# The causal mask's product on VectorE, one head later, instead of on GpSimd, in a three-stage vision kernel

## The reference

```python
x = rmsnorm(tokens, norm_w)
q = (x @ Wq)   # 16 query heads of 64
k, v = x @ Wkv # 8 key/value heads of 64: two query heads share one
q, k = l2norm(q) * (q_gamma + 1) * 8, l2norm(k) * (k_gamma + 1) * 8
sim = tanh(q @ k.T / 50) * 50 / 8
sim = where(triu(ones(n, n), 1), -max, sim)      # causal
out = softmax(sim) @ v
x1 = layernorm(tokens + out @ Wout)
```

## Time and profile before

| | us |
|---|---|
| timed runs, median of 3 (lowest, highest) | 2081.14 (2079.12, 2081.46) |
| profiled execution, its own time | 2070.81 |
| span of that execution, first to last instruction | 2069.1 |
| busy: PE, DVE, ACT, POOL | 1838.8, 1195.2, 877.6, 609.9 |

### The profile page before, as it was taken

The page is one execution under the profiler, slowest core; times in us unless marked ns, Lnnn a source line. Parts: engine busy times, 40 slices in busy tenths (PEclk is TensorE's granted clock), DMA queues, the critical chain, the costliest instruction groups (busy, mean ns, idle before and its releaser), DMA issues. The chain is left out here.

```text
span 2069.1 us, 31611 instructions
## 1 busy us (share of the span) xinstructions
PE 1838.8 (89%) x11768; PEld 1586.8 (77%) x11768; DVE 1195.2 (58%) x2023; ACT 877.6 (42%) x1076; POOL 609.9 (29%) x452
## 2 busy tenths in 40 slices
PE   3698898897987998998899899779999999999997
PEld 2598798897976877777787778668787787877876
DVE  6788878888865776777667677421341414314141
ACT  3554554544435664666367366322222222212221
POOL 3212223223150231332122122232433334333332
PEclk9799999998998999999999999889999999999999
DMA  9122311213111000200200020060000000000000
GB/s 120 54 77 97 118 75 53 89 75 145 49 44 50 22 22 9 84 22 15 77 22 15 8 70 22 8 267 1 21 21 0 20 0 20 20 0 21 1 11 11
DMA packets 32213, 95.89 MB, mean 46 GB/s; under 512 B 18630, under 2 KB 18758, under 8 KB 26569
## 3 DMA queue, kind: packets, MB, share of 16 engines
q1 hardware_dynamic: 32076, 94.00, 14.5%
HBM read 81.37 MB, written 24.15 MB: 51 GB/s over the span
## 5 line engine op out<-in xcount | busy, mean ns | idle before, releaser
L573 PE MATMUL conv<-w_hi,x_hi 128*128 128x368 f16 (+5 forms) x1320 | 355.0, 278 | 4.2 <-issue 4.0
L573 PE MATMUL conv<-w_lo,x_hi 128*128 128x368 f16 (+5 forms) x1320 | 355.7, 278 | 0.0
L573 PE MATMUL conv<-w_hi,x_lo 128*128 128x368 f16 (+5 forms) x1320 | 354.4, 278 | 0.0
L835 POOL TENSOR_TENSOR probs<-probs,mask 128x512 f32<-128x512 f32 x128 | 167.3, 1307 | 440.6 <-ACT probs L909 440.6
L1327 ACT ACTIVATE raw_c<-ring,sh 128x512 f32<-128x512 f32 x128 | 88.2, 689 | 371.3 <-PE ring L1424 371.2
L1115 PE MATMUL mixed<-v,probs 128*128 128x65 f32 x1536 | 201.6, 282 | 41.4 <-DVE parts L995 41.2
L1115 PEld LDWEIGHTS mixed<-v,probs 128*128 128x128 f32 x1536 | 185.8, 195 | 56.9 <-issue 40.2
L1289 POOL TENSOR_TENSOR ha_lo<-raw_c,ha_hi 128x512 fp32r<-128x512 f32 x128 | 165.1, 1290 | 210.0 <-DVE ha_hi L1339 210.0
L1424 PE MATMUL ring<-ha_hi,wh 128*128 128x512 f32 x512 | 208.7, 408 | 16.9 <-POOL ha_lo L1289 16.9
L1424 PE MATMUL ring<-ha_lo,wh 128*128 128x512 f32 x512 | 205.2, 401 | 0.0
L1339 DVE CAST ha_hi<-raw_c 128x512 fp32r<-128x512 f32 x128 | 80.7, 631 | 213.2 <-ACT raw_c L1327 211.0
(11 more groups left out here) (153 smaller groups left out, 3757.1 us busy)
## 6 DMA issues: line engine op xcount, KB each, us to landing
xt<-x_columns_in SPq DMA_DIRECT2D x12, 1163.0 KB, 5.2
xp<-x_patches_in SPq DMA_DIRECT2D x12, 1152.0 KB, 8.9
hidden_words<-hidden_weights_in SPq DMA_DIRECT2D x8, 1408.0 KB, 8.7
words<-hidden_words SPq DMA_DIRECT2D x32, 352.0 KB, 3.1
wh<-hidden_words SPq DMA_DIRECT2D x2, 4096.0 KB, 21.2
tokens<-total SPq DMA_DIRECT2D x4, 1024.0 KB, 4.6
lines<-tokens SPq DMA_DIRECT2D x4, 1024.0 KB, 5.5
h<-tokens SPq DMA_DIRECT2D x4, 1024.0 KB, 7.4
```

The source lines that it names most:

```text
L573: ins = pe.matmul(out, xs[:, c, RI - 1 - i:RI - 1 - i + NR, :, x].rearrange("p r g -> p (r g)"), w, start=(t == 0), stop=(t == len(terms) ...
L835: pool.tensor_tensor(diag, diag, both, ALU.mult).then_inc(s_mask, 1)
```

## The change

GpSimd no longer has a part in `score`. VectorE gets a helper `apply_mask(g, n)` with the same product on the same views, in place, and the same increment of `s_mask`. VectorE calls it for head n-1 where its list comes to `score` n (n from 1), so ahead of the normalisation of head n-2 in the same slot (behind it where n is 8, 16 or 24). The mask of the last head is applied ahead of the normalisation of head 30. Before its first step VectorE waits once for the mask tile (`s_const`).

```diff
@@ GpSimd's emit
-                    elif kind == "score":
-                        n = step[1]
-                        pool.wait_ge(s_exp, g * NH + n + 1)
-                        diag = probs[:, n % 4].rearrange("p m (b i) -> p m b i", b=3)[:, :, 0:3:2]
-                        both = mask[:].rearrange("p (m b i) -> p m b i", m=1, b=1).to_broadcast([P, 2, 2, P])
-                        pool.tensor_tensor(diag, diag, both, ALU.mult).then_inc(s_mask, 1)
@@ VectorE
             dve.memset(bits[:], 0).then_inc(s_bits, 1)
+            dve.wait_ge(s_const, 3)
...
+            def apply_mask(g, n):
+                dve.wait_ge(s_exp, g * NH + n + 1)
+                diag = probs[:, n % 4].rearrange("p m (b i) -> p m b i", b=3)[:, :, 0:3:2]
+                both = mask[:].rearrange("p (m b i) -> p m b i", m=1, b=1).to_broadcast([P, 2, 2, P])
+                dve.tensor_tensor(diag, diag, both, ALU.mult).then_inc(s_mask, 1)
+
             def emit(run, g):
                 for step in run.order:
                     kind = step[0]
+                    if kind == "score" and step[1] > 0:
+                        apply_mask(g, step[1] - 1)
+                    elif kind == "mix" and step[1] == NH - 2:
+                        apply_mask(g, NH - 1)
```

## The result

The changed kernel took 2053.89 us in the median of 4 runs (2053.35 to 2060.64), beside 2080.7 for the kernel before (four runs; the prediction had three of them): ratio 0.988, 95% interval 0.9858 to 0.9901; the two medians alone give 0.987. The kernel is faster by 1.2%. The profiled execution took 2053.72 us; the prediction had 2052.6 for it, 2063 for the median, and a range of 2052 to 2078.

The account below looks back on a forecast made before the run. TensorE's order of work plus its waits for VectorE's queue was taken to bound the attention stage. Image terms of -2.7, -5.7, -4.9, -4.9 and nothing gave -18.2 us, so median 2063; range 2052 to 2078.

Parts of the forecast that it names:

- VectorE pays for GpSimd's mask: Attention stage: a VectorE instruction meeting a GpSimd mask stands still until it ends, in the queue TensorE waits for.
- The 58 us of relief: VectorE's standing still that goes with GpSimd's masks: L998 36.5 us, L960 12.5, L954 8.9, together 58 us.
- 0.60 a mask: What each of 128 masks adds to VectorE's queue: 0.60 us, in all 77 us.
- case C: Rival: VectorE's queue gets longer, by masks above 0.60 us or relief under 23 us; 2086 at 1.215 a mask; chance 0.10.
- No new wait through the mask's place: VectorE's mask n-1 in slot n adds no wait: exp is ready, and TensorE already waits for the normalisation behind it.
- The sum: Attention stage's gains added image by image, four groups of up to four images: -18.2 us, profiled execution 2052.6.
- the steady one: Steady image, second of each group and third of the last, 5 in all: about -0.53 us each, -2.7 together.
- I take the same 18 off it: Step from profile to median: the timed median, 2081.14, 10 us above the profiled execution, also falls by 18, to 2063.
- Case A: Rival: denser TensorE work gives back a third of the granted clock's cost, 9 us lower, 2054; chance 0.15.
- Thirty-eight masks on the path: About 38 of 128 masks stand ahead of TensorE's waits, so a microsecond more per mask would cost 38.
- B: Rival: TensorE next waits for ScalarE to empty the banks; only waits at image ends are gained, 2077; chance 0.14.
- D: Rival: VectorE waits for exp at its queue's head, normalisation behind it; 0.15 x 128 = 19 us, 2082; chance 0.06.

Follow-up runs that it names:

- idle product: Changed kernel, with GpSimd also doing a mask-sized product on a spare tile nobody waits for, when exp is done: 2101.6 us, ratio 1.0103 to the kernel before.
- idle memset: Changed kernel, with GpSimd also writing zeros into a spare tile of 1408 columns when exp is done: 2072.4 us, ratio 0.9957 to the kernel before.
- mask twice: Changed kernel, with each mask done twice on VectorE, the second waiting for the first: 2119.5 us, ratio 1.0179 to the kernel before.
- mask behind: Changed kernel, with VectorE's mask behind the normalisation of the same slot instead of in front of it: 2111.8 us, ratio 1.0173 to the kernel before.
- mask at once: Changed kernel, with the mask of head n in slot n itself, one head earlier: 2143.3 us, ratio 1.0317 to the kernel before.
- second root and words: Changed kernel, with only each image's second inverse root on GpSimd and VectorE's or-ing of weight words moved to n = 4, 8, ... 32: 2029.1 us, ratio 0.9771.
- no mask: Kernel before, with the causal mask's product left out on every engine, so attention isn't causal: 2027.1 us, ratio 0.9732 to the kernel before.
- GpSimd later: Kernel before, mask still on GpSimd but started one head later, after the scores of head n+1: 2090.5 us, ratio 1.0049 to the kernel before.
- words moved: Changed kernel, with VectorE's or-ing of the weights' words at n = 4, 8, ... 32 instead of 2, 6, ... 30: 2053.6 us, ratio 0.9865.
- roots on GpSimd: Changed kernel, with both inverse roots of the heads' norms moved from VectorE to GpSimd as maximum and power: 2050.9 us, ratio 0.9863 to the kernel before.

## Why the prediction was right, and where not

**What bounds it:** TensorE's waits for VectorE's queue. Right. Each experiment with longer waits was slower than the changed kernel, and taking them away by other means (the last one) gave the largest gain that keeps the computation whole.

**VectorE pays for GpSimd's mask.** Right, and shown by the idle product, which brings the stops back with nobody waiting for it. But "an instruction of VectorE that meets a mask stands still" was too wide: in the kernel before, `parts`, which reads `mixed` in PSUM, met a mask 59 times and took 424 to 426 ns each time. And L954, which the prediction lists among the instructions with both inputs in SBUF, has one input; "idle memset" shows that it is stopped by GpSimd's writing too. The 58 us of relief came out as (0.575 - 0.292) x 128 = 36, (0.319 - 0.183) x 90 = 12 and (0.477 - 0.178) x 30 = 9.

**0.60 a mask.** Measured 0.61, in place and with a broadcast: case C's first half is out. The start before the end of the instruction ahead is seen at the mask too (0.08 us). It isn't against the Trainium skill: the section that the prediction cites ("VectorE: DVE Perf Modes", "The DRAIN you can't avoid") goes on to say that a next instruction that is not held starts earlier, which the prediction left out.

**No new wait through the mask's place.** Right for the place that was chosen: VectorE waits 12.9 us for exp in 10 places, of which 3.7 is the very first, ahead of which it had nothing to do. The other nine are of 1.0 us, at the first head of an image; only in the last image does a normalisation follow within 3 us. The prediction had found that one place, of 0.15. The two runs with another place, +57 and +88 us, show how narrow that is. The reason I gave, that TensorE's next mixture needs both the mask and the normalisation, would have allowed the place behind as well, for 8 us. What decides is that the mask stands where VectorE would wait for the mixture; the prediction saw this for masks 12 to 14 and did not make it the rule.

**The sum.** From tanh to tanh, the lengths of the four groups were 176.69, 177.49, 177.15 us and 126.8 for the last; they became 170.41, 173.65, 173.63 and 123.8. That is -6.3, -3.8, -3.5 and -3.0, forecast -5.8, -4.7, -5.3 and -2.4: together -16.6 against -18.2. By images of the second group: the first 36.39 to 38.29 (+1.90, forecast -0.92), the steady one 36.11 to 35.16 (-0.95, forecast -0.53), the third 39.97 to 38.15 (-1.82, forecast -1.65), the fourth 65.02 to 62.05 (-2.97, forecast -1.63). The first stood at the lower clock for 6.8 us where it had stood at the higher one throughout, the fourth for 6.8 instead of 10.2; so the sum came out nearer than its terms, which is luck in part. The windows of the first image, before and after:

```profile
829.57:865.96 36.39, 32.42 (x229) 27.14 (x230) 30.50 (x75) 22.80 (x31) 12.25 (x10) 1.00 0.34 118
822.83:861.12 38.29, 35.25 (x229) 29.52 (x230) 30.18 (x82) 22.80 (x30) 1.93 (x2) 0.91 0.32 112
```

The sum was also to come from waits alone. TensorE's waits for the parts were to fall from 41.2 to about 27 us and fell to 33.6; all its waits for VectorE fell by 12.2 in the stretch, its whole idle time by 13.4 (56.6 to 43.2), and the other 3.2 of the 16.6 are busy time (601.5 to 598.3). Ahead of mixture 3 of the second group, 853.30 became 846.21 with the group's start 6.74 earlier: -0.35, forecast -0.42. The profiled execution was to take 2052.6 and took 2053.7. (A slip that changes nothing: the chances of "faster" add up to 0.75 at most, not 0.76.)

**The median.** 2063 was forecast, about 2054 measured: inside the range of 2052 to 2078, but below the 2056 to 2071 that the forecast kept for itself. The step that failed is "I take the same 18 off it". The 10 us between the profiled execution and the median of before were the clock (0.954 against 0.947), and this is not a constant that both kernels carry: the changed kernel ran at 0.952 in the mean, near its profile. Case A had this at 9 us, at a chance of 0.15, with 2054 as its time, and that is what came; it was not a rival to the forecast but rode on it. That shorter waits are what raised the clock is likely by the clocks below, but no run here shows it apart.

**Thirty-eight masks on the path, 38 us for a microsecond.** The count was fair (44 by the waits of "mask twice"), the price was not: a microsecond of TensorE's waiting was followed by about as much in the clock. From the changed kernel, waits and half the low time (an estimate of its cost) against what was added to the profiled execution: idle memset +9 and +11, +17; idle product +24 and +17, +43; mask behind +25 and +24, +54; mask twice +32 and +34, +66; mask at once +48 and +37, +90. Where waits were taken away it doesn't hold: second root and words -22 and -5, -27; no mask -20 and +2, -16. The mean clock over all executions of a kernel says the same: 0.952 for the changed kernel, then with growing waits 0.948 (idle memset), 0.947 (before), 0.944 (GpSimd later), 0.943, 0.939, 0.937 and 0.934 (mask at once); with shorter waits it is 0.951 (words moved), 0.950 (roots on GpSimd), 0.952 (second root) and 0.955 (no mask). Why the clock follows the waits so closely in one direction and less in the other I can't say from these runs. Waits aren't all of it either, as the two profiles of the kernel before show (42.5 and 70.4 us low with waits of 50.3 and 51.4). And the half of the low time counts stretches in which TensorE waited anyway, so the sums are no proof of a mechanism; that more waiting comes with more low clock is what they show.

**B** (the wait moves to ScalarE) and **D** (exp) did not come about in the changed kernel; D's mechanism is real and costs 88 us one head earlier.

## What to carry to other kernels

When an engine with time to spare shares its work with a busy one, look at the busy engine's smallest instructions: a mean well above their shortest record (575 ns against 290) is another engine's work being paid for in the queue that counts, and moving that work onto the busy engine can be cheaper than leaving it. Put added work where the engine would wait for something else, in front of the wait and not behind it; here 57 us lay between the two. And do not build a forecast of a median on a single profile without looking at its granted clock: a wait added to TensorE cost itself and, in these runs, about as much again in the clock; a wait taken away gave back little more than itself.

## What the runs showed of the hardware that I had not expected

GpSimd's writing alone (a memset of 1.27 us) does not touch VectorE's products with two inputs (292 ns) but stops its maximum with one input (500 ns against 178). GpSimd's power with two inputs in SBUF, 4.19 us from 882.67, does not stop VectorE's mask at 883.85, which took its 0.68 us. Nor is it the only one: 15 masks and 45 products `o` lay wholly inside such a power, at 0.68 and 0.29 us. So not every GpSimd instruction that reads SBUF stops VectorE's products with two inputs there, as the rule cited under "idle memset" (the Trainium skill, "SBUF — State Buffer", "Who interferes with whom") would have it. The timeline of "roots on GpSimd", both engines:

```profile
882.67 4.19 POOL L837 TENSOR_TENSOR rn<-rn,neg_half 128x24 f32<-128x24 f32 x1
...
883.85 0.68 DVE L937 TENSOR_TENSOR probs<-probs,mask 128x512 f32<-128x512 f32 x1
```

And the mean granted clock of one and the same kernel lay anywhere between 0.938 and 0.954 from one execution to the next, which is 26 us from the slowest to the fastest.
